# A graph attention layer and a mixture of experts on one core: edge counts in another order, masks in one pass, later shifts

## The reference

```
e     = leaky_relu(al_s[src] + al_d[dst], 0.2)      # per edge and head, al = sums of h with two vectors
alpha = exp(e - max per dst) / (sum per dst + 1e-16)
out   = sum over edges of h[src] * alpha, h = x @ W
x1 = x + GAT2(elu(GAT1(layernorm(x))))  # GAT1: 4 heads x 512; GAT2: 1 head x 768; loops added to the edges
x2 = x1 + MoE(layernorm(x1))            # 8 experts, top 2, capacity, inner 384, plus a shared expert
```

## Time and profile before

| | us |
|---|---|
| profiled execution, its own time | 1465.73 |
| its span | 1463.9 |
| TensorE busy | 1267.5 (87%) |
| VectorE busy | 931.5 (64%) |
| ScalarE busy | 595.6 (41%) |
| GpSimd busy | 257.6 (18%) |

### The profile page before, as it was taken

How to read it: one execution, slowest core, us unless ns; L and a number is a source line. 1 busy time by engine, 2 the same in 40 slices (tenths; PEclk the granted TensorE clock), 3 DMA queues, 4 the chain that set the end, 5 groups by cost and what they waited for, 6 DMA issues and landing times.

```text
span 1463.9 us, 19131 instructions
## 1 busy us (share of the span) xinstructions
PE 1267.5 (87%) x7118; PEld 814.8 (56%) x7118; DVE 931.5 (64%) x1851; ACT 595.6 (41%) x1025; POOL 257.6 (18%) x190
## 2 busy tenths in 40 slices
PE   1574898579599789979998999999999989999996
PEld 1342344334355455445456888888854746666664
DVE  6477997599788968988963456254478624333340
ACT  1344224566475546547842066200231134444441
POOL 1399300000000000000000000130011543443322
PEclk9987899899899989989998999999899989999999
DMA  8442201413441453114045611251310286767622
GB/s 209 153 161 76 78 0 34 144 51 95 114 131 38 113 157 90 40 36 117 30 134 187 187 58 57 75 149 32 97 66 1 62 240 175 187 174 173 164 58 29
DMA packets 71438, 152.66 MB, mean 104 GB/s; under 512 B 10837, under 2 KB 34901, under 8 KB 70730
## 3 DMA queue, kind: packets, MB, share of 16 engines
q1 hardware_dynamic: 64699, 134.28, 30.4%
q0 software_dynamic: 6656, 17.26, 6.1%
HBM read 118.93 MB, written 34.59 MB: 105 GB/s over the span
## 4 chain that ended last, share of the span: by engine, by line
PE 60%; DVE 17%; DMA 6%; ACT 6%; issue 5%; POOL 5%; SPq 1%; DVEq 0%; POOLq 0%; ACTq 0%
PE PS L1654 40%; PE PS L1771 10%; PE PS L1717 5%; DVE sb L1299 3%; POOL sb L774 3%; DVE sb L1320 2%; DVE sb L1328 2%; PE PS L1766 2%; DVE sb L1208 1%; DVE sb L1335 1%; DMA sb<-in_x_dram 1%; DVE sb L1251 1%; POOL sb L806 1%; DMA sb<-in_L_ffn_w_dram 1%; DVE sb L1371 1%
## 5 line engine op out<-in xcount | busy, mean ns | idle before, releaser
L1654 PE MATMUL PS<-sb,sb 128*125 128x384 f16 (+8 forms) x4404 | 790.1, 340 | 68.0 <-DVE sb L1213 23.4
L1654 PEld LDWEIGHTS PS<-sb,sb 128*125 128x125 f16 (+3 forms) x4404 | 543.7, 129 | 302.0 <-issue 70.7
L1771 PE MATMUL PS<-sb,sb 125*128 125x375 f16 (+1 forms) x1440 | 267.4, 347 | 0.0
L1771 PEld LDWEIGHTS PS<-sb,sb 125*128 125x128 f16 x1440 | 141.9, 99 | 121.9 <-issue 14.0
L786 POOL TENSOR_TENSOR sb<-sb,sb 125x768 f32<-125x768 f32 x10 | 18.0, 1841 | 784.4 <-DMA sb<-in_x_dram 784.4
L931 ACT ACTIVATE sb<-sb 125x375 f32<-125x375 f32 (+1 forms) x150 | 81.6, 544 | 116.1 <-DVE sb L1320 115.6
L1498 DVE SCALAR_TENSOR_TENSOR sb<-sb,sb 128x2304 f16<-128x2304 f32 x27 | 68.8, 2557 | 89.0 <-ACT sb L1066 89.0
L1717 PE MATMUL PS<-sb,sb 125*125 125x500 f16 x320 | 88.6, 417 | 12.6 <-DVE sb L1251 12.6
L1251 DVE TENSOR_SCALAR sb<-sb,sb 125x500 f16<-125x500 f16 x320 | 95.5, 380 | 3.3 <-PE PS L1717 3.2
L1320 DVE SCALAR_TENSOR_TENSOR sb<-sb,sb,sb 125x375 f32<-125x375 f32 (+1 forms) x150 | 95.3, 637 | 1.8 <-ACT sb L925 1.6
L925 ACT ACTIVATE sb<-sb,sb 125x375 f32<-125x375 f32 (+1 forms) x150 | 93.7, 628 | 3.9 <-DMA sb<-aa_d 3.9
(11 more groups left out here) (190 smaller groups left out, 1122.8 us busy)
## 6 DMA issues: line engine op xcount, KB each, us to landing
sb<-in_L_ffn_w_dram SPq DMA_DIRECT2D x24, 1152.0 KB, 5.7
sb<-xt_d SPq DMA_DIRECT2D x40, 375.0 KB, 3.7
sb<-in_L_gnn_W_dram SPq DMA_DIRECT2D x32, 384.0 KB, 3.2
sb<-mask_d SPq DMA_DIRECT2D x20, 546.9 KB
sb<-h_d SPq DMA_DIRECT2D x10, 1000.0 KB, 5.5
h_d<-sb SPq DMA_DIRECT2D x16, 375.0 KB, 6.8
sb<-aa_d SPq DMA_DIRECT2D x5, 1093.8 KB
sb<-in_L_gnn_W_dram SPq DMA_DIRECT2D x18, 256.0 KB, 3.6
```

What stands on the lines that cost most here:

```text
L1654: ins = M(out_, lhs(a), rhs(b), start=first and a + b == 0, stop=last and a == 1)
L1771: ins = M(PS[:, t, 0:n], hb[:, i, pa, 128 * c:128 * c + 128], P[:, i, pb, lo:lo + n], start=i == 0 and pa + pb == 0, stop=i == NT - 1 and ...
```

## The change

- **Counting.** The edges are walked tile by tile (170 tiles of 125). Each tile gets one one-hot instruction for the one or two chunks that it can meet (500 or 1000 elements); there are 54 tiles with one chunk and 116 with two, 286 matmuls in all. The loops over nodes are no longer counted but added as an identity afterwards (two VectorE instructions). The code is unrolled, PSUM has four banks in turn, and the ring has 8 tiles.
- **Early part.** The first T0 = 24 tiles (39 matmuls) are counted between the transposes of the first five tiles of x, ahead of the norm of the third piece.
- **Source one-hots.** GpSimd subtracts (10 instructions, 2250 elements a partition, from the start on) and VectorE compares with zero (10 instructions).
- **First projection.** The order of its tiles is 7, 8, 9, 0 to 6; the first three stay in their buffers and are not loaded again.
- **v2.** The products of 5 chunks run before, those of 11 chunks after the low parts of head 1's weights; ScalarE sums 6 of them under the projection, 16 under the counting (after three of four chunks from c = 4 on) and 10 after tile 3 of `proj(1)`. Four product buffers instead of two. A2R and WV are loaded only after the last transpose of x. `load_v2(15)` on SyncE stands ahead of the mask stores.
- **Masks.** One pass: Relu of 1e30 minus 1e30 times the count, and the maximum subtracts it.
- **Heads.** `SHIFT_AT` is 10 instead of 8, the next head's steps begin at g = 11 instead of 10, and the lists of steps are changed to match.
- **Experts.** The first `down` of an expert waits part by part.

```
-    RO, RG, PG = 12, 4, 2
+    RO, RG, PG = 8, 2, 2
...
+            def source_onehots(q):
+                a, b = OLP * q, min(OLP * (q + 1), KA)
+                dve.wait_ge(s_od, q + 1)
+                V.tensor_scalar(OL[:, a:b, :], OL[:, a:b, :], 0.0, None, ALU.is_equal).then_inc(s_ol, 1)
+
+            def pair_onehots(tiles):
+                for t in tiles:
+                    if t >= RO and t % RG == 0:
+                        dve.wait_ge(s_cm, t - RO + RG)
+                    c, w = met[t][0], len(met[t])
+                    V.tensor_scalar(OR[:, t % RO, 0:w, :], iok[:, 0:w, :], float(SP * c), KEY[:, t:t + 1], ALU.add,
+                                    ALU.is_equal).then_inc(s_or, 1)
+
+            piece(0)
+            piece(1)
+            for i in range(XF):
+                xt_lo(i)
+                if i < 2:
+                    source_onehots(i)
+                pair_onehots(range(T0 * i // XF, T0 * (i + 1) // XF))
+            piece(2)
+            for i in range(XF, NT):
+                xt_lo(i)
+
+            for q in range(NT):
+                h_lo(0, q)
+                if q >= 2:
+                    source_onehots(q)
...
+            pool.wait_ge(s_slo, 1)
+            for i in range(NT):
+                a, b = OLP * i, min(OLP * (i + 1), KA)
+                nc.gpsimd.tensor_tensor(OL[:, a:b, :], iot[:, :].unsqueeze(1).to_broadcast([T, b - a, T]),
+                                        SLO[:, a:b].unsqueeze(2).to_broadcast([T, b - a, T]), ALU.subtract
+                                        ).then_inc(s_od, 1)
...
+            def counts(tiles):
+                for t in tiles:
+                    if t % OLP == 0:
+                        pe.wait_ge(s_ol, t // OLP + 1)
+                    if t % PG == 0:
+                        pe.wait_ge(s_or, min(t + PG, ET))
+                    for w, c in enumerate(met[t]):
+                        if t == reach[c][0] and c >= 4:
+                            pe.wait_ge(s_ce, c - 3)
+                        ins = M(PS[0:T, c % 4, 0:KC], OL[:, t, :], OR[:, t % RO, w, :], start=t == reach[c][0],
+                                stop=t == reach[c][1] - 1)
+                    ins.then_inc(s_cm, 1)
...
+            for c in range(NC):
+                act.wait_ge(s_cm, reach[c][1])
+                A(CT[:, :, c * DC:c * DC + DC], PS[0:T, c % 4, 0:KC].rearrange("p (i n) -> p i n", n=DC), ACT.Copy,
+                  accum_out=CS[:, c:c + 1]).then_inc(s_ce, 1)
+                if c >= 4 and c % 4 < 3:
+                    v2_sum(summed)
+                    summed += 1
...
-                  ACT.Relu, bias=1.0, scale=-1.0).then_inc(s_act, 1)
-                act.wait_ge(s_act, j + 1)
-                A(MSK[:, j % 2, :], MSK[:, j % 2, :], ACT.Copy, scale=NEG).then_inc(s_mm, 1)
+                  ACT.Relu, bias=big[:, :], scale=NEG).then_inc(s_mm, 1)
...
-        PJ_STEPS = [2, 1, 1, 0]
-        CUR_STEPS = [[3, 3, 2, 2, 2, 2, 2, 2, 0, 0, 0, 0, 0, 0, 0],
+        PJ_STEPS = [[0, 0, 0, 0, 2, 2, 2, 2, 2, 2], [1] * NT, [1] * NT]
+        CUR_STEPS = [[3, 3, 2, 2, 2, 2, 2, 2, 2, 0, 0, 0, 0, 0, 0],
...
-        NEXT_STEPS = [[0, 0, 0, 0, 0, 0, 0, 0, 0, 0, 1, 2, 2, 2, 2],
-                      [0, 0, 0, 0, 0, 0, 0, 0, 0, 0, 1, 2, 2, 2, 2],
-                      [0, 0, 0, 0, 0, 0, 0, 0, 0, 0, 2, 2, 3, 3, 3]]
+        NEXT_STEPS = [[0, 0, 0, 0, 0, 0, 0, 0, 0, 0, 0, 2, 2, 2, 2],
+                      [0, 0, 0, 0, 0, 0, 0, 0, 0, 0, 0, 2, 2, 2, 2],
+                      [0, 0, 0, 0, 0, 0, 0, 0, 0, 0, 0, 3, 3, 3, 3]]
...
-        ROW_AT, SHIFT_AT = 1, 8
+        ROW_AT, SHIFT_AT = 1, 10
...
+                        if made is not None and q == 0:
+                            pe.wait_ge(s_sg, made + KI)
+                            pe.wait_ge(s_alo, made + m + 1)
+                        elif made is not None:
+                            pe.wait_ge(s_gx, made + KI)
```

More of the change, by code:

```diff
@@ L622, in _ @@
                         load_w1_rows(h + 2, range(2, KD))
+                    store_h1(NB * h)
                     chain_shift(h + 1)
@@ L1006, in _ @@
                         h_hi(h + 1, i)
-                        p_steps(h, PJ_STEPS[h])
+                        if h == 0 and i == NT // 3:
+                            for k in range(summed, 2 * NCH):
+                                v2_sum(k)
+                        p_steps(h, PJ_STEPS[h][i])
                 else:
@@ L1187, in norm, with piece @@
                 link(V.tensor_scalar(SD[:, a:b], SD[:, a:b], SX, None, ALU.mult))
-            for n, (a, b) in enumerate(PIECES):
+            def piece(n):
+                a, b = PIECES[n]
                 dve.wait_ge(s_x[n], 32)
@@ L1412, in _ @@
                         chain_shift_rows(h + 1)
+                    if h == 0 and g == CH:
+                        v2_split()
                     p_steps(h, cur // 2)
@@ L1664, in _, with x_T @@
             ins.then_inc(s_once, 1)
-            for i in range(NT):
+            def x_T(i):
                 pe.wait_ge(s_xn, i + 1)
```

295 lines of the change are left out of this document (136 added, 159 removed).

## The result

The kernel after takes 1459.59 us (median of 8 runs, 1457.34 to 1468.45), the kernel before 1467.15 us in the same comparison (1465.81 to 1474.97). The ratio is 0.9947, with a 95% interval from 0.9929 to 0.9964: 7.8 us faster, where 26 were forecast. The time lies inside the wide range (1390 to 1466) and outside the forecast case's own, 1425 to 1455. The profiled execution took 1458.8 us, its span is 1457.0 and the mean clock 0.932 (before 0.947).

A forecast was written before the change was run, and what follows sets the result against it. VectorE and GpSimd were taken to set the pace up to 242 us, TensorE in the heads. Terms -23.8 + 1.3 - 6 + 5.3 + 5 - 7.8 = -26 took 1465.73 to 1440 us; range 1390 to 1466.

The forecast's parts named there:

- forecast case: Whole kernel: the prediction's main case, 1440 us, its own range 1425 to 1455, chance 0.46.
- Step 1: Up to x's last transpose: GpSimd's differences and VectorE's bursts hinder each other; 83 us, bounds 54 and 92.
- Step 2: First projection: tiles 4.2 us apart against 8.1 before, ten in 42 us; counting resumes at 129.5 instead of 141.2.
- Step 3: Counting: 53 us for the engines, 11 for GpSimd's pairs, 22 for products; 86 us, to 215.5 against 239.3 before.
- Step 4: End of counting and masks: identity additions add about 1.3 us; masks take 25 instead of 31, a gain of 6.
- Step 5: Rest of v2, after head 0's shift: ten sums and six products make tile 4 late; cost 5.3 us, bounds 0 and 10.
- Step 6: Shifts in the heads: shift row copied 8 to 10 us later; 5 us slower over three heads, bounds -28 and +15.
- Step 7: Down products of the experts: two parts run under the wait for the third; 7.8 us won, between 0 and 11.6.
- The sign that was to show the prediction wrong: Head 0's attention (before: 317 us) starting before 270 or after 315 would make the prediction wrong.
- Rival B: Heads: the later shift pays in full, 33 us better than the forecast's +5, time 1407; chance 0.18.
- Rival A: Front: GpSimd does not hinder VectorE, another 55 us gained, 1385, or 1413 for half; chance 0.20 with its half.
- Rival C: Front: shared memory side starves TensorE and its clock falls; counting 115 us, time 1478, slower; chance 0.12.

The follow-up runs named there:

- a_copies: Kernel after with ScalarE's copies of chunks 0 to 2 moved ahead of the high parts of head 1's weights: 1445.16 us, ratio 0.9831 to the kernel before.
- b_mask: Kernel before with the one-pass mask alone: 1462.53 us, ratio 0.9946.
- b_shift10: Kernel before with the shift part alone (shift transposes at group 10 instead of 8, next head's P steps from group 11): 1477.37 us, ratio 1.0054.
- a_shift8: Kernel after with the shift back at group 8, step lists and mask store as before: 1451.82 us, ratio 0.9867 to the kernel before.
- a_pj: Kernel after with the shift back at group 8 and head 0's own P steps as before: 1454.62 us, ratio 0.9903 to the kernel before.
- a_v2dve: Kernel after with all 32 v2 products and sums made by VectorE in one instruction each: 1444.56 us, ratio 0.982 to the kernel before.
- a_diffdve: Kernel after with source one-hots made by VectorE alone, without GpSimd's differences: 1442.31 us, ratio 0.9811 to the kernel before.
- c_late_v2: Kernel after with early chunk copies, shift at 8, v2 on VectorE, GpSimd differences for groups 2 to 9 only after x's last transpose, in pieces: 1415.67 us, ratio 0.9651.

## Why the prediction was wrong

The sign was right; the size was not. At the profiled execution's own scale 19 us are missing (26 against 6.9), and the steps of the prediction account for them so:

- **Step 1** (last transpose of x, 83): 79.6, by luck: two errors cancel. GpSimd's difference takes 3.9 us, not 5, but a VectorE instruction stood behind every single one, even those of 125 x 2 elements, where I had let a burst hold and GpSimd wait. So GpSimd was done at 48.6 us and not at 73.5, with 10 of the 42 VectorE instructions behind a difference, and the 24 one-hots and the norm of the third piece ran unhindered after it. The Trainium skill (SBUF — State Buffer, SBUF: two separate sides) has the lock held for a whole instruction, the other side blocked. The trace agrees for this stretch (3.43 us for 125 x 2 elements), and the literal reading, which I had put at 92 us with differences of 5 and one for each of the 42, is right in kind. What I took as evidence against it is the same lock held by the other side: a stream of VectorE instructions without a gap keeps GpSimd out, as the product of 21.1 us shows too. Where GpSimd was at work when VectorE came they took turns, where a VectorE stream was already running GpSimd waited for its end; what decides this no run here isolates.
- **Step 2** (42 us): 40.5 for the ten tiles, and the counting resumes at 125.0, 4.5 earlier than put (3.4 of them from step 1). Right.
- **Step 3** (86 us, to 215.5): 96.8, to 221.7. This is the first step that failed. Two of its terms had the right size: 53 us for the two engines alone (53.85 measured without v2) and 22 for the products (24 measured, though not as the sum of their durations: 9 of it are matmuls at the lower clock, and most of the rest waits for one-hots and for a bank). What failed is the third: not 11 us for six pairs but a stall of 19.25, since I followed GpSimd's and VectorE's orders but not ScalarE's, where the weights' high parts, and SyncE's loads behind `chain_row`, stand ahead of the first chunk copies. The wait was readable from the order alone; a_copies takes it away. The clock over the counting was 0.78, where the prediction's sign was above 0.8.
- **Step 4** (25 us of masks, from the first mask transpose to L1305): 26.2, and to the shift transpose, 0.9 us later, 27.2; alone (b_mask) 25.5 to the shift transpose against 32.2 before. Right.
- **Step 5** (+5.3): from the shift to head 0's attention 46.5 us instead of 42.9: +3.6. But against the kernel without v2 (36.4) it is 10, and v2 costs this kernel 35 us in all. In the kernel before the products stood under the slow projection (8.1 us a tile); that the change moved their cost more than it removed it is likely but not shown, as no run leaves v2 out of the kernel before.
- **Step 6** (+5): 14 by the traces of after, of which the shift is 7 to 8 (b_shift10, a_shift8), about 5 are work that head 0 makes later (a_pj), and 2 stay open. The shift alone is near the +5; what the step left out is the later P steps of head 0, and in its mechanism two things. I had the copy of the shift row 8 to 10 us later and the 9.6 us of DMA kept, and both came: in b_shift10 the copy is at 396.9 instead of 388.2, with the attention 0.5 us earlier, and the first P step 9.4 behind it. The signs came too (3.8 us at the shift transposes of the heads, 11.6 at the next projections). Missed was first that with the shift at 8 the work of groups 8 to 10 covers this DMA on VectorE, and at 10 nothing does: VectorE waits about 9.5 us for it in each head, while its waits for TensorE fall from 17.0 to 3.0. The second is the clock. TensorE's saved wait comes back ahead of the next projection and the P tiles, in more and smaller pieces, and 36.5 instead of 18.1 us of its work fall to the lower level: its busy time goes from 406.7 to 416.4 us for the same matmuls.
- **Layer 2** starts 3.5 us earlier than before and is level (830.1 against 830.5) at its own shift; these 3 us more of small waits I didn't trace further.
- **Step 7** (-7.8): -8.4 alone (5 to 12), with 7.0 us less of waiting. Right.

By position: 6 us were missing at the end of the counting, 9 more in the heads and 4 behind them, most of these in layer 2. The sign that was to show the prediction wrong, head 0's attention before 270 or after 315, did not catch this: it starts at 299.6, since the largest miss lies behind it. Rival B falls: undoing the shift helps. Rival A falls too: GpSimd hinders throughout, and the kernels in which it does less (a_v2dve, a_diffdve) are 19 and 20 us faster than after. Rival C did not come, though its trait did: the clock was 0.50 in the stall and 0.67 from 185 to 205 us:

```profile
125.00:145.00 20.00, 1.06 (x2) 0.25 (x2) 4.90 (x6) 2.81 (x5) 12.64 (x11) 0.50 0.52 160
...
185.00:205.00 20.00, 10.81 (x31) 5.13 (x30) 15.21 (x17) 7.39 (x20) 18.73 (x9) 0.67 0.27 81
```

## What to carry to other kernels

When a step is moved, walk every in-order queue past its new place, the quiet engine's too: the 19 us stall was on ScalarE, which was busy for 40% of the span. A long wait of the busiest engine can be another engine's lag, as here; moving the wait doesn't shorten it, and it may uncover a DMA round trip that the lag had hidden, so ask what the lagging engine does during that trip. And work of two engines that take turns adds up, so giving it to the idle one of the two may be no relief: both times that GpSimd's part of the kernel after went to VectorE, the kernel became faster. Where it stands matters, though: c_late_v2 gives eight groups back to GpSimd beside the projection and is no slower.

## What the runs showed of the hardware

- VectorE and GpSimd took strict turns by instruction in the early part, for VectorE's scalings and comparisons in SBUF of any size (3.43 us for 125 x 2 elements), but batch statistics ran at 0.54 us beside them; with pieces of 1.4 us a one-hot of 0.26 took 1.5.
- Where a VectorE stream was already running there were no turns: one GpSimd product took 21.1 us instead of 1.81, most of it under 88 one-hots that ran at 0.41 each, and it was done 1.7 us after the last of them.
- A multiply-and-sum of 768 float32 elements takes VectorE 0.95 us; the product on GpSimd takes 1.81 and its sum on ScalarE 0.84.
- A difference of 2250 float16 elements takes GpSimd 3.94 us (4.26 with a normed tile in VectorE's turn), 1.75 ns an element, against 2.36 for its float32 product; VectorE makes the same one-hots alone in 2.49 us.
- With the same matmuls and the same idle time in the heads (45.6 and 47.3 us), waits in more and smaller pieces put 36.5 instead of 18.1 us of TensorE's work on the lower clock level and cost 9.7 us of busy time.
